# Second attention: one relu instruction over both PSUM banks of a pair, 128x2x256, with one wait and one signal, instead of one for each bank

## The chip, the cores and the metric

The kernel runs on one core of one Trainium2 chip. The metric is the time of one execution on the device in microseconds (us); lower is better. In this document TensorE is the matmul engine (PE in the rows, PEld its weight loads), VectorE is DVE, ScalarE is ACT, GpSimd is POOL and SyncE is SP. PSUM is the memory that matmuls write; its unit here is a bank, 512 fp32 values on each of 128 partitions.

## The reference, cut to what matters

Four layers run one after another on x of shape 16 x 512 x 128, each as x = x + layer(layernorm(x)): a first attention (causal, without softmax), a mixture-of-experts layer, a second attention, and the experts again. The change lies in the second attention, which begins like this:

```python
Q = proj(wq, bq); K = proj(wk, bk); V = proj(wv, bv)      # 16 heads of 8
scores = jnp.einsum('bhqd,bhkd->bhqk', Q, K) * scale       # 512 x 512 for each head
top_u = jax.lax.top_k(scores.max(axis=-1), u)[1]           # u = 6 queries of each head
```

Only the six queries with the largest row maximum go on to softmax and context. Nearly all the work of the stage is therefore the row maximum of 16 sequences x 16 heads x 512 queries over 512 keys.

## The kernel before, in words

Every engine has an instruction stream of its own, written out by hand; streams meet only at semaphore waits. The second attention runs `body` once for each of the 16 sequences b, and in it 32 steps n, one for each pair of (128 queries, two heads). A step uses one tile `pair[n % RING]` of two PSUM banks q = 0, 1, with RING = 3; a tile is used again three steps later. One step is:

- TensorE, `scores` (L1937 to L1948): for each bank q it waits until VectorE has signalled that bank's earlier content as read (`bmax_done`, three steps back), then writes 512 columns with a matmul on 32 rows of the array (L1947) and signals `bsc_done`. An fp32 matmul is two instructions in the profile, so a step has four.
- What lies in the two halves of a bank: the keys of `kTs` from column HALF on are 256 columns of k2 and then 256 columns of k1 - k2 (POOL makes the differences, L684). So the first half of a bank holds the scores of half of the keys, and the second half the differences of the other half's scores to them. The maximum of two scores is then first + relu(difference).
- ScalarE, `first_half_above` (L955 to L959): for each bank it waits for `bsc_done`, writes the relu of the second half (128x256) into the SBUF tile `rel[n % RING][:, q, :]` and signals `relu_done`. In the rows `rel` has the name pT, which is the memory it lies in.
- VectorE, `largest` (L1433 to L1441): for each bank it waits for `relu_done`, adds the first half of the bank and `rel`, takes the maximum along the row (L1439, two instructions in the profile: the custom reduction and the read of its accumulator into `smax`), and signals `bmax_done`, which frees the bank for TensorE.

Between the steps each stream has other work of the same and of neighbouring sequences at fixed places n. Those that matter here:

- VectorE: `residual` of an earlier sequence at n = 0 (L1497) and `route_ranks` after n = 3 (its last instruction writes `rank`, L1131).
- TensorE: after n = 5 `turn_largest`, which transposes the row maxima (L1953) and waits for `rank`; after n = 9 `project_q` (L1930); after n = 14 `select_x` (L1966); after n = 16 `select_q` (L1971); after n = 18 `selected_scores` (L1975); after n = 20, 22, 23, 24, 25, 26 and 29 seven more pieces (L1935, L1980, L1662, L1986, L1668, L1991, L1995); after n = 31 `scatter_context` (L2001).
- ScalarE: `largest` after n = 5 (L939), `masked_q` after each of n = 10 to 13 (L922, 128x512), `selected_x` after n = 14 (L948), and others.

The first body has no previous sequence and the last two no next one to work for, so these pieces are partly missing there; `each_four` strings the bodies together without a pause.

Of the kernel before, what the change touches and what calls it, by code (L numbers as in the profile page):

```python
# [10 lines left out]
ACT = mybir.ActivationFunctionType  # L11
# [11 lines left out]
SEQ = 512  # L23
# [24 lines left out]
RING = 3  # L48
PAIRS = TB * H // 2
HALF = SEQ // 2  # L50
# [9 lines left out]
def build(nc, w, out):  # L60
    ctx = ExitStack()
    with ctx:
# [6 lines left out]
        def sem(name):  # L69
            return ctx.enter_context(nc.semaphore(name))  # L70
# [140 lines left out]
        rel = [t[:, :, :].rearrange("p (q a) b -> p q (a b)", q=2) for t in pT[4:4 + RING]]  # L211
# [19 lines left out]
        pair = [ctx.enter_context(nc.psum_tensor(f"pair{i}", [P, 2, 512], F32)) for i in range(RING)]  # L231
# [13 lines left out]
        s = {n: sem(n) for n in names.split()}  # L245
# [534 lines left out]
        def _(act):  # L780
# [173 lines left out]

            def first_half_above(b, n):  # L955

                for q in range(2):
                    act.wait_ge(s["bsc_done"], 2 * (b * PAIRS + n) + q + 1)
                    act.activation(rel[n % RING][:, q, :], pair[n % RING][:, q, HALF:SEQ], ACT.Relu).then_inc(s["relu_done"], 1)  # L959

            def body(b, u, h, x, last=True, next=True, fetch=True, before=True):
                for n in range(PAIRS):
                    first_half_above(b, n)
                    if last and n == 5:
                        largest(b - 1)
                    if next and n == 7:
                        turned(b + 1 + B, "att", xnT)
                    if next and 10 <= n < 14:
                        masked_q(b + 1, 1 - h, range(n - 10, n - 9))
                    if last and n == 14:  # L970
                        selected_x(b - 1)
                    if last and n == 20:
                        selected_exp(b - 1)
                    if next and n == 20:
                        keys(b + 1, 1 - h)
                    if last and n == 22:
                        turned_exp(b - 1)
                    if before and n == 23:
                        turned(b - 2 + B, "ffn", xfT)
                    if last and n == 24:  # L980
                        context_x(b - 1)
                    if before and n == 26:
                        route_exp(b - 2 + B)
# [43 lines left out]
        def _(dve):  # L1027
# [405 lines left out]
            def largest(b, h, n):  # L1433

                t, j, a = n // (H // 2), n % (H // 2) // 2, n % 2
                for q in range(2):
                    dve.wait_ge(s["relu_done"], 2 * (b * PAIRS + n) + q + 1)
                    head = (2 * a + q) * GH + j
                    dve.tensor_tensor_reduce(out=rel[n % RING][:, q, :], in0=pair[n % RING][:, q, 0:HALF], in1=rel[n % RING][:, q, :],  # L1439
                                             scale=1.0, scalar=LOWEST, op0=ALU.add, op1=ALU.max,  # L1440
                                             accum_out=smax[h][:, t, head:head + 1]).then_inc(s["bmax_done"], 1)  # L1441
# [58 lines left out]
            def body(b, u, h, x, last=True, next=True, fetch=True, before=True):  # L1500
                for n in range(PAIRS):
                    largest(b, h, n)
                    if before and n == 0:
                        residual(b - 2)
# [664 lines left out]
```

## Time and profile before

| | us |
|---|---|
| median of 3 runs | 1378.17 |
| lowest and highest of the 3 runs | 1370.37 and 1379.9 |
| the profiled execution, its time | 1371.3 |
| the profiled execution, first to last instruction (span) | 1369.4 |
| second attention in it, first score matmul to last maximum | 480.67 to 1107.3 |

The profiled execution has 1.9 us outside its span. The page of the profile gives busy times of each engine, the chain of work that ended last, and the costliest groups of instructions. "Idle before" is the time in which an engine stood still just before an instruction, and the name behind the arrow is what ended it. Times in rows are us from the start of the span unless marked ns. A granted TensorE clock of 1.00 in a row is the full 2.4 GHz.

### The profile page before, as it was taken

What the parts mean: (1) busy time and instruction counts of PE and PEld (TensorE: products, weight loads), DVE (VectorE), ACT (ScalarE), POOL (GpSimd) and SP (SyncE); (2) the same over time, 40 slices, a digit from 0 to 9 for tenths busy, and PEclk for the clock granted to TensorE, in tenths of its full rate; (3) what the DMA queues carried; (4) which work ended last, traced back from release to release, by engine and by line L of the source; (5) the groups of instructions that cost most, each with busy time, mean ns of one, the idle gap of its engine ahead of it and who ended that gap; (6) DMA issues with size and microseconds to landing.
All of it is one profiled execution on the core that took longest, in us unless ns stands there. A gap on an engine that the chain in (4) does not pass through costs nothing.

```text
span 1369.4 us, 28269 instructions
## 1 busy us (share of the span) xinstructions
PE 1232.1 (90%) x8494; PEld 779.4 (57%) x8494; DVE 1040.6 (76%) x4462; ACT 759.4 (55%) x1907; POOL 832.5 (61%) x1238
## 2 busy tenths in 40 slices
PE   5999999999999999999999999999999999899100
PEld 2666655567898855545444545444454479799100
DVE  3899998996665478898999889989997756566322
ACT  3455443445756677675666677656666556556000
POOL 3247776677625134566777777767774445467776
PEclk9999999999999989998999899999999899999655
DMA  6855502013556400000101001020000125476522
GB/s 187 277 178 189 167 29 86 29 46 119 185 159 213 131 28 17 17 22 26 30 25 29 28 24 32 28 89 26 26 28 15 41 83 168 151 212 205 147 76 75
DMA packets 118695, 124.75 MB, mean 91 GB/s; under 512 B 15504, under 2 KB 108816, under 8 KB 118544
## 3 DMA queue, kind: packets, MB, share of 16 engines
q1 hardware_dynamic: 102160, 89.37, 20.6%
q0 software_dynamic: 16384, 33.59, 8.5%
q8 instruction: 68, 1.11, 0.3%
q14 instruction: 83, 0.68, 0.2%
HBM read 49.63 MB, written 73.27 MB: 90 GB/s over the span
## 4 chain that ended last, share of the span: by engine, by line
PE 74%; DVE 11%; POOL 5%; issue 4%; ACT 2%; DMA 2%; SPq 0%; ACTq 0%; POOLq 0%; DVEq 0%
PE pair L1947 26%; PE pair L1856 9%; POOL vmyg L585 5%; PE pair L1719 5%; PE bank L1743 4%; PE pair L1867 4%; DVE pT L1439 4%; PE pair L1845 2%; PE pair L1708 2%; PE bank L1668 2%; PE bank L1662 2%; PE pair L1689 1%; PE bank L1966 1%; PE pair L1729 1%; PE bank L1986 1%
## 5 line engine op out<-in xcount | busy, mean ns | idle before, releaser
L1947 PE MATMUL pair<-kT,apart 32*128 32x512 f32 x2048 | 460.2, 673 | 3.9 <-DVE smax L1439 2.5
L1439 DVE CUSTOM_DVE_ANT_0 pT<-pair,pT 128x256 f32<-128x256 f32 x1024 | 383.8, 416 | 76.0 <-ACT pT L959 70.8
L959 ACT ACTIVATE pT<-pair 128x256 f32<-128x256 f32 x1024 | 327.5, 397 | 197.5 <-PE pair L1947 194.5
L1947 PEld LDWEIGHTS pair<-kT,apart 32*128 32x128 f32 x2048 | 192.1, 191 | 127.9 <-DVE smax L1439 79.9
L585 POOL DMA_INDIRECT vmyg<-ybufA,slg x128 | 124.1, 969 | 100.0 <-DVE smax L1439 62.3
L1856 PE MATMUL pair<-xeT,unit_w 128*128 128x256 f32 x752 | 180.8, 384 | 0.0
L585 POOL DMA_INDIRECT vmyg<-ybufB,slg x128 | 122.7, 959 | 71.2 <-DVE smax L1439 33.5
L546 POOL DMA_INDIRECT dispB<-xnf,sli x128 | 128.5, 1004 | 57.1 <-issue 34.9
L546 POOL DMA_INDIRECT dispA<-xnf,sli x128 | 129.9, 1015 | 51.5 <-issue 30.1
L1152 DVE TENSOR_TENSOR pT<-pair,causal 128x1024 f32<-128x1024 f32 x128 | 151.2, 1213 | 12.9 <-PE pair L1719 12.1
L1322 DVE TENSOR_TENSOR hid<-sg,pair 128x512 f32<-128x512 f32 x96 | 64.8, 675 | 120.6 <-ACT sg L876 120.4
L1856 PEld LDWEIGHTS pair<-xeT,unit_w 128*128 128x128 f32 x752 | 137.5, 193 | 15.2
L1351 DVE SCALAR_TENSOR_TENSOR xs<-vmyg,wts,xs 128x128 f32<-128x128 f32 x248 | 80.8, 377 | 66.6 <-DMA vmyg<-ybufB,slg 55.1
L1867 PE MATMUL pair<-unit_w,hid 128*128 128x128 f32 x752 | 100.4, 276 | 7.3 <-DVE ye L1331 7.3
L1867 PEld LDWEIGHTS pair<-unit_w,hid 128*128 128x128 f32 x752 | 97.9, 191 | 15.8 <-DVE hid L1322 6.7
L883 ACT ACTIVATE unit_w<-f_w 128x384 f32 x156 | 73.2, 515 | 49.9 <-PE pair L1867 47.7
L876 ACT ACTIVATE sg<-pair 128x512 f32<-128x512 f32 x96 | 56.6, 589 | 50.4 <-PE pair L1856 50.0
L1439 DVE DVE_READ_ACCUMULATOR2_ANT smax<- 128x1 f32 x1024 | 82.5, 81 | 0.0
L1719 PE MATMUL pair<-apart,kT 32*128 32x512 f32 x512 | 77.6, 651 | 1.7 <-DVE pT L1152 1.7
L1331 DVE COPY ye<-pair 128x512 f32<-128x512 f32 x96 | 64.5, 672 | 8.8 <-PE pair L1867 5.2
L1743 PE MATMUL bank<-pT,vmyg 128*32 128x128 f32 x2048 | 70.7, 280 | 0.0
L483 POOL TENSOR_SCALAR lnv<-mv 128x4 f32<-128x4 f32 (+1 forms) x51 | 12.0, 235 | 87.9 <-DVE mv L1050 85.7
(232 smaller groups left out, 1946.1 us busy)
## 6 DMA issues: line engine op xcount, KB each, us to landing
dispB<-zeros SPq DMA_DIRECT2D x16, 1408.0 KB
apart<-dispA SPq DMA_DIRECT2D x94, 128.0 KB
apart<-dispB SPq DMA_DIRECT2D x94, 128.0 KB
ybufA<-ye SPq DMA_DIRECT2D x46, 256.0 KB
ybufB<-ye SPq DMA_DIRECT2D x46, 256.0 KB
dispA<-zeros SPq DMA_DIRECT2D x33, 128.0 KB
xs<-in_x SPq DMA_DIRECT2D x16, 256.0 KB, 3.1
out<-xs SPq DMA_DIRECT2D x15, 256.0 KB, 2.6
```

What stands on the lines that cost most here:

```text
L546: pool.indirect_dma_start(out=area, out_offset=bass.IndirectOffsetOnAxis(ap=sli[h][:, K * j + k:K * j + k + 1], axis=0), in_=xnf[g % NF][: ...
L585: pool.indirect_dma_start(out=yg[h][:, j, :], out_offset=None, in_=ybuf[second(g)], in_offset=bass.IndirectOffsetOnAxis(ap=slg[h][:, j:j + ...
L883: last = act.activation(unit_w[g % NX][:, u, :], f_w[:, bass.ds(ex[u], 1), :].rearrange("p a n -> p (a n)"), ACT.Copy)
L959: act.activation(rel[n % RING][:, q, :], pair[n % RING][:, q, HALF:SEQ], ACT.Relu).then_inc(s["relu_done"], 1)
L1152: dve.tensor_tensor(pTd[n % NG][:, :, :], pair[1 + n % 2][:, :, :].rearrange("p q (j t) -> p (q j) t", j=GH), causal[:, :].unsqueeze(1).to ...
L1351: last = dve.scalar_tensor_tensor(out=xb, in0=yg[h][:, K * j + k, :], scalar=wts[:, bass.ds((b * TB + j) * K + k, 1)], in1=xb, op0=ALU.mul ...
L1439: dve.tensor_tensor_reduce(out=rel[n % RING][:, q, :], in0=pair[n % RING][:, q, 0:HALF], in1=rel[n % RING][:, q, :], scale=1.0, scalar=LOW ...
L1719: pe.matmul(bank[4 + g][:, :].rearrange("p (j t) -> p j t", j=GH), kTs[h][at, c * P:(c + 1) * P], apart[h][at, :, c * P:(c + 1) * P], star ...
L1743: last = pe.matmul(bank[1][at:at + QG, c * P:(c + 1) * P], vm[:, c, j * P + at:j * P + at + QG], pT[c % 2 * NG + g][:, j, :], start=(c == ...
L1856: last = pe.matmul(bank[3 + 2 * h + k][:, u * UR:(u + 1) * UR], unit_w[r][:, u, k * D:(k + 1) * D], xeT[h][:, UT * u:UT * (u + 1), :].rear ...
L1867: last = pe.matmul(bank[7][:, j * D:(j + 1) * D], hid[h][:, j, :], unit_w[r][:, j // UT, 2 * D:3 * D], start=True, stop=True)
L1947: pe.matmul(pair[n % RING][:, q, :], apart[h][at, j, t * P:(t + 1) * P], kTs[h][at, HALF:], start=True, stop=True).then_inc(s["bsc_done"], 1)
```

## The change

On ScalarE the two waits and two activations of a step become one wait for both banks (`bsc_done` at its second count) and one activation over both banks, 128 partitions x 2 x 256, with one signal. On VectorE the wait for `relu_done` moves out of the loop over q: one wait for the step, then the two reductions. `relu_done` counts steps in place of banks. Nothing else changes: matmuls, reductions, `bmax_done` for each bank and the ring of three stay as they are.

```diff
             def first_half_above(b, n):
 
-                for q in range(2):
-                    act.wait_ge(s["bsc_done"], 2 * (b * PAIRS + n) + q + 1)
-                    act.activation(rel[n % RING][:, q, :], pair[n % RING][:, q, HALF:SEQ], ACT.Relu).then_inc(s["relu_done"], 1)
+                act.wait_ge(s["bsc_done"], 2 * (b * PAIRS + n) + 2)
+                act.activation(rel[n % RING][:, :, :], pair[n % RING][:, :, HALF:SEQ], ACT.Relu).then_inc(s["relu_done"], 1)
...
             def largest(b, h, n):
 
                 t, j, a = n // (H // 2), n % (H // 2) // 2, n % 2
+                dve.wait_ge(s["relu_done"], b * PAIRS + n + 1)
                 for q in range(2):
-                    dve.wait_ge(s["relu_done"], 2 * (b * PAIRS + n) + q + 1)
                     head = (2 * a + q) * GH + j
```

## Rows read from the trace of the kernel before

**Rows 1.** The page: span, and each engine's busy us, share, instructions.

```profile
span 1369.4 us, 28269 instructions
...
PE 1232.1 (90%) x8494; PEld 779.4 (57%) x8494; DVE 1040.6 (76%) x4462; ACT 759.4 (55%) x1907; POOL 832.5 (61%) x1238
```

**Rows 2.** Busy time by engine in one steady body: PE, PEld, DVE, ACT, POOL, clock.

```profile
706.70:744.98 38.28, 38.19 (x198) 19.24 (x197) 35.00 (x193) 26.28 (x78) 28.41 (x39) 1.00 0.10 28
```

**Rows 3.** Waits over 0.15 us, whole second attention: total us, times, longest.

```profile
ACT pT L959 <- PE pair L1947: 194.5, 210, 4.3
...
PEld pair L1947 <- DVE smax L1439: 79.9, 157, 2.0
...
DVE pT L1439 <- ACT pT L959: 70.8, 100, 3.1
```

**Rows 4.** The same wait of VectorE in the first body and the last.

```profile
DVE pT L1439 <- ACT pT L959: 7.5, 12, 1.6
...
DVE pT L1439 <- ACT pT L959: 10.8, 11, 3.1
```

**Rows 5.** ScalarE's instructions by shape: busy us, mean ns, idle before.

```profile
L959 ACT ACTIVATE pT<-pair 128x256 f32<-128x256 f32 x1024 | 327.5, 397 | 197.5 <-PE pair L1947 194.5
...
L876 ACT ACTIVATE sg<-pair 128x512 f32<-128x512 f32 x92 | 55.0, 598 | 45.9 <-PE pair L1856 45.4 <-issue 0.2
...
L876 ACT ACTIVATE sg<-pair 128x256 f32<-128x256 f32 x4 | 1.5, 384 | 4.5 <-PE pair L1856 4.5
```

**Rows 6.** Timeline at n = 0 of that body: start, us, engine, line.

```profile
707.85 1.48 ACT L959 ACTIVATE pT<-pair 128x256 f32<-128x256 f32 x4 [1.76 <-PE pair L1947]
708.27 0.42 DVE L1439 CUSTOM_DVE_ANT_0 pT<-pair,pT 128x256 f32<-128x256 f32 x1 [0.54 <-ACT pT L959]
...
708.62 0.42 DVE L1439 CUSTOM_DVE_ANT_0 pT<-pair,pT 128x256 f32<-128x256 f32 x1
```

**Rows 7.** Chain that ended last, between n = 3 and n = 6.

```profile
712.21 0.23 DVE rank L1131
...
712.49 0.60 PE bank L1953 x4
```

**Rows 8.** Timeline at n = 6.

```profile
714.18 1.21 ACT L959 ACTIVATE pT<-pair 128x256 f32<-128x256 f32 x4 [0.46 <-PE pair L1947]
...
714.60 0.42 DVE L1439 CUSTOM_DVE_ANT_0 pT<-pair,pT 128x256 f32<-128x256 f32 x1 [0.80 <-ACT pT L959]
```

**Rows 9.** Timeline, ScalarE and VectorE, at n = 10 and 11.

```profile
718.69 0.66 ACT L959 ACTIVATE pT<-pair 128x256 f32<-128x256 f32 x2 [1.52 <-PE pair L1947]
...
719.24 0.78 ACT L922 ACTIVATE apart<-bank,qbias,inturn 128x512 f32<-128x512 f32 x1
...
719.90 0.67 ACT L959 ACTIVATE pT<-pair 128x256 f32<-128x256 f32 x2
...
720.33 0.42 DVE L1439 CUSTOM_DVE_ANT_0 pT<-pair,pT 128x256 f32<-128x256 f32 x1
```

**Rows 10.** Timeline at n = 14 and 15.

```profile
722.21 0.38 PE L1966 MATMUL bank<-pT,xnb 128*128 128x128 f32 x1
...
724.45 1.21 ACT L959 ACTIVATE pT<-pair 128x256 f32<-128x256 f32 x4
...
724.87 0.42 DVE L1439 CUSTOM_DVE_ANT_0 pT<-pair,pT 128x256 f32<-128x256 f32 x1
```

**Rows 11.** Timeline at n = 19.

```profile
728.97 1.21 ACT L959 ACTIVATE pT<-pair 128x256 f32<-128x256 f32 x4 [1.54 <-PE pair L1947]
729.38 0.42 DVE L1439 CUSTOM_DVE_ANT_0 pT<-pair,pT 128x256 f32<-128x256 f32 x1
```

**Rows 12.** Timeline at n = 26 and at the next body's n = 0.

```profile
738.86 0.66 ACT L959 ACTIVATE pT<-pair 128x256 f32<-128x256 f32 x2 [1.39 <-PE pair L1947]
...
739.27 0.43 DVE L1439 CUSTOM_DVE_ANT_0 pT<-pair,pT 128x256 f32<-128x256 f32 x1 [0.88 <-ACT pT L959]
...
746.56 0.42 DVE L1439 CUSTOM_DVE_ANT_0 pT<-pair,pT 128x256 f32<-128x256 f32 x1 [0.54 <-ACT pT L959]
```

## The prediction

> **What bounds the kernel now.** The page first: 1369.4 us of span, VectorE busy 76% of it and ScalarE 55% [rows 1]. These are averages over four layers, so the second view is one body of the second attention alone. In its 38.28 us TensorE shows 38.19 busy at the full granted clock, VectorE 35.00 and ScalarE 26.28 [rows 2]. VectorE is nearly full and ScalarE is not (69%). TensorE's figure must not be taken as a bound: two steps that have their banks ready share the array, so the same work could take less.
>
> The third view, the waits, shows a ring. TensorE's weight loads waited 79.9 us for VectorE's maxima (a bank not yet read), ScalarE waited 194.5 us for score matmuls, and VectorE 70.8 us, 100 times, for the relu [rows 3]. So a bank goes matmul, relu, reduction and back, and each engine in it at times waits for the one before. The view has no other wait of VectorE. Whether such a standstill lies on the path that sets the end has to be read place by place, and that is done below.
>
> **What the change does to one step.** It removes 512 activations, waits and signals on ScalarE and 512 waits on VectorE; it adds no matmul, reduction or transfer. VectorE's two reductions stay .35 us apart [rows 6], which is the reduction and its accumulator read, so the wait taken away there gives nothing.
>
> The new instruction, 128x2x256, is not in the trace. Nearest are two shapes on one line, 128x256 at 384 ns and 128x512 at 598 ns; today's relu, 397 ns on average, is the first shape [rows 5]. The 256 further elements cost 598 - 384 = 214 ns. I take .60 us. From above it is bounded by the .66 that two relus take today [rows 9], and if a second bank cost as much as a second instruction, by 2 x .385 = .77; from below by .385 + .21, since the elements are all still read.
>
> First effect, a gain: on ScalarE a step holds the engine from 718.69 until the next instruction begins at 719.24, .55 us [rows 9]. The second of two activations starts before the first has ended: two of .385 to .40 take .66, so some .12 overlap. The new one lets the next start after .60 - .12 = .48 to .49, so .06 is saved in each step.
>
> Second effect, a loss: today the first reduction starts .42 after the first relu (707.85 to 708.27 [rows 6]; the same at n = 6, 15, 19 and 26 [rows 8, 10 to 12]), while the second relu runs beside it. Now it starts .60 + .03 after the instruction begins: **.21 later**. Where VectorE releases the two banks .35 apart and the matmuls follow at that distance, the one wait for both banks adds that .35 too.
>
> The trace shows ScalarE unsaturated and VectorE waiting for it. The Trainium skill, Perfetto Trace Analysis, section Optimizing Scalar/DVE Operations, says that grouping into larger operations helps if the engine is saturated, and that if ScalarE or VectorE aren't saturated but cause bubbles on other engines, breaking instructions up may let work complete sooner. By the first half the kernel would gain ScalarE's time, by the second it would lose what is worked out below; the rows show the second case.
>
> **Where .21 counts.** I follow one body from its n = 0 (VectorE 708.27) to the next n = 0 (746.56 [rows 12]), 38.29 us, and ask at each wait what released it, and how far that has moved already.
>
> 1. n = 0: VectorE waits .54 [rows 6] for matmuls that stand behind `scatter_context`. Late: .21. From here VectorE works without a real pause to `rank`, which releases TensorE's L1953 [rows 7].
> 2. n = 6: its matmuls follow L1953 directly; VectorE waits .80 [rows 8]. Total .42.
> 3. n = 11: the second reduction of n = 6 frees the bank for n = 9, after it come `project_q` and n = 10, whose relu starts at 718.69 after an idle 1.52. Then ScalarE itself is the bound: relu, `masked_q`, relu [rows 9]. Here .06 is gained, so .15 is added. Total .57. At n = 12 to 14 ScalarE gains further, but by then VectorE, moved by .57, is itself the later one.
> 4. n = 15: the second reduction of n = 11 frees the bank for n = 14, behind it stands `select_x` (722.21), behind that n = 15, whose relu starts at 724.45 [rows 10]. Total .78.
> 5. n = 19: the reductions of n = 15 free the banks of n = 18, then `selected_scores`, then n = 19, for which ScalarE had been idle 1.54 [rows 11]. VectorE started just as the relu ended, so all .21 is late. Total .99.
> 6. n = 26: the second reduction of n = 19 frees n = 22; after that TensorE is the bound, with another piece after nearly every step, and VectorE waits .88 [rows 12]. Total 1.20. The reductions of n = 26 to 28 free the banks of n = 29 to 31, `scatter_context` follows, and the ring closes at the next n = 0.
>
> So a body becomes 5 x .21 + .15 = **1.20 us** longer, 3%. Eleven bodies are of this kind (the fourth to the fourteenth): 11 x 1.20 = 13.2 us.
>
> The other five miss some of this work. By the waits view the first has 12 waits of VectorE for the relu and the last 11 [rows 4], the three between them 7, 5 and 10: 45 of the 100. The eleven have 55, and 13.2 / 55 = .24 us for each; 45 x .24 = 10.8. Sum **24.0 us**. A second count agrees roughly: 100 waits x .21 = 21.
>
> No other queue is passed by anything that moves. POOL's gathers and scatters are released by VectorE's maxima, so they shift with the bodies; experts before and after are untouched.
>
> The profiled execution took 1371.3 us, 1.9 beyond its span: 1371.3 + 24.0 = **1395.3 us**. Its time lies 6.9 below the median shown (1378.17); against that the same sum would be 1402.
>
> **The rivals.**
>
> *Hidden anyway.* VectorE is busy 35.00 of 38.28 [rows 2], and most steps reach it with the relu long done; if the matmul order sets the pace, lateness ends in the next wait. For it: only 100 of 512 steps show a wait over .15 [rows 3]. Against: the waits are released by matmuls that themselves waited for VectorE, so they move along. If only the crossings at n = 0 and n = 6 hold: 16 x .42 = 6.7, so 1378 us; if none, 1371.
>
> *Faster: ScalarE is the bound at n = 10 to 13.* There .06 is gained in four steps of 15 bodies: 15 x 4 x .06 = 3.6 us, 1367.7. It decides if all first-bank lateness is hidden and VectorE still follows ScalarE at n = 14. Even .06 in all 512 steps would give only 31 us, and ScalarE's 194.5 us of waiting [rows 3] exclude most of that. The Trainium skill, ScalarE: Activation LUTs, section What ACT_TABLE_LOAD costs, gives 186 ns + 0.833 ns for each element and about 93 ns of overlap; by it one instruction saves 93 ns against two, an estimate of 48 us of ScalarE time in all. The trace agrees on the slope (214 ns for 256).
>
> *Slower by far: the ring runs in step.* Where no other work lies between, the banks are released .35 apart, and each turn through three steps pays .21 + .35 = .56. If all 100 waits paid that: 56 us, 1427. The first body has such a stretch; in the eleven others the waits that count follow a piece of TensorE work, after which both banks start together.
>
> *The instruction is dearer.* At .66 a crossing costs .275, at .77 it costs .385: 24.0 x .275 / .21 = 31, 1402; 24.0 x .385 / .21 = 44, 1415.
>
> **How the numbers follow.** My forecast, with its bounds on the instruction's price (1395 to 1415), has .72; hidden anyway .17; in step .07; faster through ScalarE .04. The range goes from 1378 (two crossings a body) to 1415 (the dear instruction). A measurement of this kernel can tell about 1% from no change, 14 us. Slower by more: nearly all of the forecast and the in-step case, .76. Within: hidden anyway, the gain of ScalarE (3.6 us is 0.3%), and a forecast half as large, .20. Faster by over 1% needs a gain of 14 us that no row shows: .04.
>
> **What would show it.** Right: the new instruction at about .60 us; the body of 38.28 at about 39.5; VectorE's waits for the relu longer and more often, with the first reduction .63 after the relu starts; ScalarE's busy time for L959 down from 327.5 to about 307. TensorE's waits for VectorE's maxima go up as well. Wrong: bodies of 38.3 us, in which the longer wait is paid back by a shorter one at the next place; or a VectorE that waits no longer than today, since the relu then came early enough.

## The result and the profile after

The changed kernel took 1413.49 us (median of 4 runs, 1411.02 to 1426.4), the kernel before 1379.04 in the same comparison (4 runs, 1370.37 to 1382.7). The ratio is 1.0294, 95% interval 1.0251 to 1.0337: slower by 2.5 to 3.4%, and by 34.5 us if the medians are compared, which is the lower end of that. Ratios, here and below, leave out the few runs that took over 1.5% longer than the fastest of their kernel; medians are of all runs. The forecast was slower, 1395.3 us. That is 24.0 above the profiled execution before but only 16 above the median of 1379.04, so against the median the loss was about twice the forecast.

The page of the changed kernel, first its span and the busy time of each engine, then the three groups of the ring (line, engine, operation, busy us and mean ns, idle before):

```profile
span 1413.9 us, 27757 instructions
...
PE 1276.8 (90%) x8494; PEld 796.6 (56%) x8494; DVE 1043.5 (74%) x4462; ACT 730.7 (52%) x1395; POOL 830.9 (59%) x1238
...
L1946 PE MATMUL pair<-kT,apart 32*128 32x512 f32 x2048 | 497.4, 708 | 4.4 <-DVE smax L1438 2.9
L1438 DVE CUSTOM_DVE_ANT_0 pT<-pair,pT 128x256 f32<-128x256 f32 x1024 | 387.1, 417 | 115.3 <-ACT pT L958 112.2
L958 ACT ACTIVATE pT<-pair 128x512 f32<-128x512 f32 x512 | 296.3, 601 | 271.3 <-PE pair L1946 270.0
```

The new instruction takes 601 ns, as estimated from [rows 5]. ScalarE is busy 28.7 us less than before (759.4 [rows 1] to 730.7) and waits more. Its time for this line is 296.3 us and not the 307 forecast: 512 instructions of 601 ns would be 308, but some overlap. VectorE's work is the same; its wait for the relu has grown from 70.8 us [rows 3] to 112.2. The waits view of the second attention counts how often (total us, times, longest):

```profile
ACT pT L958 <- PE pair L1946: 270.0, 312, 4.3
DVE pT L1438 <- ACT pT L958: 112.2, 141, 3.0
PEld pair L1946 <- DVE smax L1438: 86.5, 165, 1.5
```

The windows view gives the first three bodies and one later body (length, then busy us of PE, PEld, DVE, ACT, POOL, then the granted TensorE clock as a share of 2.4 GHz, the DMA engines' busy share and GB/s):

```profile
482.61:521.54 38.93, 38.32 (x136) 20.43 (x137) 26.39 (x140) 21.59 (x37) 13.40 (x16) 0.69 0.08 21
521.54:563.59 42.05, 41.40 (x180) 21.36 (x180) 31.64 (x161) 25.70 (x46) 14.97 (x17) 0.84 0.05 13
563.59:605.11 41.52, 41.04 (x194) 20.28 (x193) 35.12 (x188) 24.49 (x46) 18.91 (x23) 0.96 0.05 14
850.85:890.63 39.78, 39.58 (x198) 19.59 (x197) 35.02 (x194) 24.55 (x46) 28.57 (x40) 1.00 0.09 27
```

The last line answers to [rows 2]: at the full clock a body takes 39.78 us in place of 38.28, 1.5 more (1.20 was forecast). The first lines show what the forecast has no word of. The same three bodies in the kernel before:

```profile
480.67:513.89 33.22, 32.96 (x136) 18.11 (x137) 25.81 (x140) 24.37 (x69) 13.42 (x16) 0.85 0.09 24
513.89:550.10 36.21, 35.22 (x180) 19.08 (x180) 31.29 (x161) 27.21 (x79) 15.10 (x17) 1.00 0.06 16
550.10:588.23 38.13, 38.05 (x193) 19.21 (x192) 34.26 (x188) 26.31 (x78) 18.95 (x23) 1.00 0.06 15
```

They took 33.22, 36.21 and 38.13 us, with clocks of 0.85, 1.00 and 1.00; now they take 38.93, 42.05 and 41.52, and TensorE ran a good part of them at half clock (1.2 GHz). The whole stage grew by 42.8 us, from 626.6 to 669.4.

Within the body at full clock the crossings (the places where a late relu makes VectorE start later) can be read one by one. The timeline at its n = 0, n = 6 and the next body's n = 0:

```profile
852.06 0.60 ACT L958 ACTIVATE pT<-pair 128x512 f32<-128x512 f32 x1 [1.60 <-PE pair L1946]
852.69 0.42 DVE L1438 CUSTOM_DVE_ANT_0 pT<-pair,pT 128x256 f32<-128x256 f32 x1 [0.80 <-ACT pT L958]
...
858.65 1.08 ACT L958 ACTIVATE pT<-pair 128x512 f32<-128x512 f32 x2 [0.51 <-PE pair L1946]
859.28 0.42 DVE L1438 CUSTOM_DVE_ANT_0 pT<-pair,pT 128x256 f32<-128x256 f32 x1 [1.01 <-ACT pT L958]
...
892.48 0.42 DVE L1438 CUSTOM_DVE_ANT_0 pT<-pair,pT 128x256 f32<-128x256 f32 x1 [0.80 <-ACT pT L958]
```

From the start of the relu to the reduction it is .63 now (852.06 to 852.69) against .42 [rows 6]: the forecast .21. VectorE's wait at n = 0 went from .54 to .80, at n = 6 from .80 to 1.01 [rows 6, 8], though what comes before had already moved. Measured from the start of the first relu of the body, VectorE's first reduction shifted by:

| place | forecast, total | measured, total |
|---|---|---|
| n = 0 | .21 | .21 |
| n = 6 | .42 | .47 |
| n = 11 | .57 | .66 |
| n = 15 | .78 | .92 |
| n = 19 | .99 | 1.18 |
| n = 26 | 1.20 | 1.43 |

The steps are the ones named, but most are .25 to .26 and not .21. Where the other .04 to .05 lies is seen at n = 26, where nothing but one step's four matmuls stands before the relu. First the kernel before, then the changed one:

```profile
737.70 1.13 PE L1947 MATMUL pair<-kT,apart 32*128 32x512 f32 x4
738.86 0.66 ACT L959 ACTIVATE pT<-pair 128x256 f32<-128x256 f32 x2 [1.39 <-PE pair L1947]
```

```profile
883.09 1.13 PE L1946 MATMUL pair<-kT,apart 32*128 32x512 f32 x4
884.29 0.60 ACT L958 ACTIVATE pT<-pair 128x512 f32<-128x512 f32 x1 [1.46 <-PE pair L1946]
```

The matmuls take 1.13 in both. The relu follows their start after 1.16 (738.86 - 737.70) before and 1.20 (884.29 - 883.09) now. Only what the relu waits for has changed: both banks in place of the first (one_wait below, with narrow relus, has 1.20 too). So the wait for the second bank costs .04, and a crossing costs .21 + .04.

### The profile page after: what moved, and what is told of

It reads as the page before. It is cut to its first block, busy times and chain, and to the rows that moved or that the text cites. A ratio compares the mean times of both kernels' runs of the same rounds, so it can differ in the third digit from the quotient of the medians.

```text
span 1413.9 us, 27757 instructions
## 1 busy us (share of the span) xinstructions
PE 1276.8 (90%) x8494; PEld 796.6 (56%) x8494; DVE 1043.5 (74%) x4462; ACT 730.7 (52%) x1395; POOL 830.9 (59%) x1238
## 4 chain that ended last, share of the span: by engine, by line
PE 74%; DVE 11%; POOL 4%; issue 4%; ACT 3%; DMA 2%; SPq 1%; ACTq 0%; POOLq 0%; DVEq 0%
PE pair L1946 28%; PE pair L1855 8%; PE pair L1718 5%; POOL vmyg L585 4%; PE bank L1742 4%; PE pair L1866 4%; DVE pT L1438 3%; PE pair L1844 2%; PE bank L1667 2%; PE pair L1707 2%; PE bank L1661 2%; PE pair L1688 1%; PE bank L1965 1%; DVE xs L1350 1%; PE bank L1974 1%
## 5 line engine op out<-in xcount | busy, mean ns | idle before, releaser
L1946 PE MATMUL pair<-kT,apart 32*128 32x512 f32 x2048 | 497.4, 708 | 4.4 <-DVE smax L1438 2.9
L1438 DVE CUSTOM_DVE_ANT_0 pT<-pair,pT 128x256 f32<-128x256 f32 x1024 | 387.1, 417 | 115.3 <-ACT pT L958 112.2
L958 ACT ACTIVATE pT<-pair 128x512 f32<-128x512 f32 x512 | 296.3, 601 | 271.3 <-PE pair L1946 270.0
L1946 PEld LDWEIGHTS pair<-kT,apart 32*128 32x128 f32 x2048 | 205.7, 201 | 146.7 <-DVE smax L1438 86.5
L1151 DVE TENSOR_TENSOR pT<-pair,causal 128x1024 f32<-128x1024 f32 x128 | 151.3, 1214 | 13.2 <-PE pair L1718 12.6
```

What stands on the lines that cost most here:

```text
L958: act.activation(rel[n % RING][:, :, :], pair[n % RING][:, :, HALF:SEQ], ACT.Relu).then_inc(s["relu_done"], 1)
L1151: dve.tensor_tensor(pTd[n % NG][:, :, :], pair[1 + n % 2][:, :, :].rearrange("p q (j t) -> p (q j) t", j=GH), causal[:, :].unsqueeze(1).to ...
L1946: pe.matmul(pair[n % RING][:, q, :], apart[h][at, j, t * P:(t + 1) * P], kTs[h][at, HALF:], start=True, stop=True).then_inc(s["bsc_done"], 1)
```

## Experiments

The theory after this: (a) the late first reduction, .25 a crossing at six places of a body, is the change's direct cost; (b) the half clock is a cost of its own. Rivals: the wait for both banks, the wide instruction as such, a fixed cost for each step, and for (b) chance.

All are shown as edits of the kernel before, if not said otherwise. The ratio of each is to runs of the kernel before taken beside it, whose medians lay between 1371.68 and 1379.04 us. "Stage" is the length of the second attention in the profiled execution and its mean granted clock. "At full clock" is worked out as stage x (1 - .69 x (1 - clock)). The factor comes from the kernel before, from the body after the one in [rows 2], the next one, and the stretch in them at half clock:

```profile
744.98:785.89 40.91, 40.82 (x198) 20.34 (x198) 36.08 (x198) 26.21 (x78) 29.84 (x41) 0.90 0.10 30
785.89:825.13 39.24, 39.12 (x199) 19.63 (x198) 34.16 (x189) 26.11 (x78) 27.74 (x38) 0.97 0.08 25
777.70:787.90 10.20, 10.20 (x40) 4.99 (x38) 6.78 (x47) 3.33 (x12) 5.47 (x6) 0.50 0.08 27
```

The two bodies hold 10.2 us at half clock and took 40.91 + 39.24 in place of 2 x 38.30, 3.55 us more, so about .35 us for each us at half clock. A mean clock c means 2 x (1 - c) of the time at half clock, and 2 x .345 is the .69. The factor was measured at one place of the body; as will be seen at joint_first_three, the last column is good to some 3 us.

| kernel | median us | ratio to before (95%) | body at clock 1.00 | stage, clock | stage at full clock |
|---|---|---|---|---|---|
| before | 1379.04 | | 38.28 | 626.6, .956 | 607.6 |
| changed | 1413.49 | 1.0294 (1.0251 to 1.0337) | 39.78 | 669.4, .911 | 628.3 |
| before_again | 1376.89 | 1.0002 (.9965 to 1.0040) | 38.29 | 635.1, .936 | 607.1 |
| one_signal | 1413.85 | 1.0264 (1.0208 to 1.0320) | 39.96 | 672.2, .912 | 631.4 |
| one_wait | 1387.05 | 1.0105 (1.0033 to 1.0177) | 38.56 | 637.8, .938 | 610.5 |
| joint_short | 1374.10 | .9987 (.9956 to 1.0018) | 38.29 | 642.1, .921 | 607.1 |
| joint_at_waits | 1418.64 | 1.0344 (1.0279 to 1.0409) | 40.11 | 671.2, .915 | 631.8 |
| joint_elsewhere | 1381.87 | 1.0059 (1.0023 to 1.0096) | 38.40 | 636.7, .941 | 610.8 |
| joint_first_three | 1396.75 | 1.0208 (1.0154 to 1.0263) | 38.29 (later ones) | 647.6, .921 | 612.3 |
| joint_later | 1404.77 | 1.0232 (1.0166 to 1.0297) | 40.10 | 654.3, .948 | 630.8 |
| grouped | 1341.35 | .9766 (.9720 to .9812) | 36.97 | 595.4, .977 | 586.0 |
| grouped_joint | 1377.36 | 1.0017 (.9985 to 1.0050) | 38.30 | 632.1, .956 | 612.9 |
| turn_early | 1375.38 | .9960 (.9910 to 1.0010) | 37.98 | 618.5, .953 | 598.4 |
| grouped_spread | 1340.51 | .9780 (.9739 to .9820) | 36.97 | 595.3, .980 | 587.1 |

**before_again.** No edit.

> The kernel before, unchanged, to see how much of the time moves with the granted clock when nothing is changed. If the lower granted clock of the changed kernel (0.916 over the span against 0.939 in the profiled run before) belongs to the change: clock 0.935 to 0.945, 1370 to 1383 us, bodies of 38.3 us at full clock. If it is chance from run to run: clocks down to 0.91 here as well, and times up to about 1400 us.

Ten runs lay between 1368.63 us (clock over the span .939) and 1383.19 (.924): 14.6 us for .015 of mean clock, 9.7 for each .01. So the profiled execution of the kernel before, 1371.3 at .939, was among its fastest. The changed kernel's four runs had .905 to .925, median .919, against .931 here: below, with hardly an overlap. (The .931 itself lies below the .935 to .945 expected.) The lower clock belongs to the change and isn't chance. At 9.7 us for each .01 it makes some 12 of the 34.5 us.

**one_signal.**

```diff
 for q in range(2):
     act.wait_ge(s["bsc_done"], 2 * (b * PAIRS + n) + q + 1)
-    act.activation(...).then_inc(s["relu_done"], 1)
+    done = act.activation(...)
+done.then_inc(s["relu_done"], 1)
...
+dve.wait_ge(s["relu_done"], b * PAIRS + n + 1)
 for q in range(2):
-    dve.wait_ge(s["relu_done"], 2 * (b * PAIRS + n) + q + 1)
```

> VectorE's half of the change alone: two relu instructions, each with its own wait, but only the second one signals, and VectorE waits once for a step. The first reduction then starts .66 + .03 after the first relu begins, .27 late in place of .21, and ScalarE saves nothing. Theory 'late first reduction': at least as slow as the changed kernel, bodies at full clock 39.8 to 40.5 us, 1411 to 1435 us, granted clock over the span 0.90 to 0.92. Rival 'wait for both banks' and rival 'wide instruction' (the loss comes from ScalarE waiting for the second bank, or from reading two banks in one instruction): near the kernel before, 38.3 to 38.7 us a body, 1371 to 1390 us.

A later body at full clock (columns as in the windows above):

```profile
731.29:771.25 39.96, 39.76 (x198) 19.63 (x198) 35.43 (x194) 26.44 (x78) 28.63 (x39) 1.00 0.09 27
```

39.96 us, 1.7 more than before and .2 more than the changed kernel, with two narrow instructions and a wait for each bank. The reduction starts .69 after the relu in place of .42, .27 late, and six times .27 is 1.6. The whole loss comes without the wide instruction, from the late signal alone.

**one_wait.**

```diff
+act.wait_ge(s["bsc_done"], 2 * (b * PAIRS + n) + 2)
 for q in range(2):
-    act.wait_ge(s["bsc_done"], 2 * (b * PAIRS + n) + q + 1)
     act.activation(...).then_inc(s["relu_done"], 1)
```

> ScalarE's wait alone: it waits for both banks before the first relu, then runs two relu instructions with a signal each, and VectorE waits for each bank as before. Theory 'late first reduction': at the places that count both banks' matmuls end together, so bodies stay at 38.3 to 38.5 us; only stretches in which the banks come .35 apart lose, 2 to 8 us in all: 1372 to 1388 us, clock 0.93 to 0.94. Rival 'wait for both banks': most of the loss is here, 39.5 us a body, 1400 us or more. Rival 'wide instruction': no change.

```profile
672.92:711.48 38.56, 38.47 (x198) 19.30 (x197) 35.01 (x194) 26.30 (x78) 28.61 (x40) 1.00 0.10 29
```

.27 a body, a little above the expected 38.3 to 38.5: six crossings at .04 to .05, the wait for the second bank seen above. The wait for both banks is a sixth of the loss and not the most of it.

**joint_short.** The changed kernel with 2 x 128 columns in its instruction; the relu of the other columns is left out.

```diff
-act.activation(rel[n % RING][:, :, :], pair[n % RING][:, :, HALF:SEQ], ACT.Relu).then_inc(s["relu_done"], 1)
+act.activation(rel[n % RING][:, :, 0:P], pair[n % RING][:, :, HALF:HALF + P], ACT.Relu).then_inc(s["relu_done"], 1)
```

> The changed kernel with its one instruction cut to 2 x 128 columns, so that it takes as long as one relu before (.385); the relu of the other half of the columns is left out. One wait, one instruction and one signal over two banks remain, only the lateness is gone. Theory 'late first reduction': bodies of 38.0 to 38.4 us, granted clock back at 0.935 or more, 1365 to 1382 us. Rivals 'wait for both banks' and 'wide instruction' (one instruction over two banks does the harm): 39.5 us a body or more and 1395 us or more still. If the clock falls for a reason of its own, it stays at 0.92 here and the time is 1385 to 1395 us.

Its relu group, and a body at full clock:

```profile
L958 ACT ACTIVATE pT<-pair 128x256 f32<-128x256 f32 x512 | 187.3, 385 | 331.0 <-PE pair L1946 330.5
```

```profile
588.02:626.31 38.29, 38.20 (x199) 19.30 (x198) 35.05 (x194) 18.17 (x46) 27.77 (x38) 1.00 0.09 25
```

With one instruction over two banks, but as short as one relu before, the loss is gone: 38.29. That it is gone to the last hundredth is luck, for two effects cancel. The wait for both banks is still there, and the body should be as long as that of one_wait, 38.56. It isn't, because ScalarE's time counts at one place, n = 10 and 11, where a relu, `masked_q` and the next relu stand in a row. First one_wait, then joint_short (start, us, and VectorE's first reduction of n = 11):

```profile
685.06 0.66 ACT L959 ACTIVATE pT<-pair 128x256 f32<-128x256 f32 x2 [1.49 <-PE pair L1947]
686.27 0.67 ACT L959 ACTIVATE pT<-pair 128x256 f32<-128x256 f32 x2
686.70 0.42 DVE L1439 CUSTOM_DVE_ANT_0 pT<-pair,pT 128x256 f32<-128x256 f32 x1 [0.22 <-ACT pT L959]
```

```profile
600.16 0.38 ACT L958 ACTIVATE pT<-pair 128x256 f32<-128x256 f32 x1 [1.77 <-PE pair L1946]
601.10 0.38 ACT L958 ACTIVATE pT<-pair 128x256 f32<-128x256 f32 x1
601.52 0.42 DVE L1438 CUSTOM_DVE_ANT_0 pT<-pair,pT 128x256 f32<-128x256 f32 x1
```

The relu of n = 11 follows that of n = 10 after 1.21 us in one_wait and after .94 here: .27 gained, and VectorE no longer waits there. So of the 8.1 us less of ScalarE's time in the body (18.17 against 26.28 [rows 2]) .27 are worth something, and the rest nothing. The width of the instruction costs nothing by itself: from its start to the reduction it is .42, as before.

**joint_at_waits and joint_elsewhere.** The wide instruction in some steps only, VectorE waiting for each bank as before.

```diff
+if n in WAITED:   # 0, 6, 11 to 15, 17 to 19, 25 to 27; "not in" for joint_elsewhere
+    act.wait_ge(s["bsc_done"], 2 * (b * PAIRS + n) + 2)
+    act.activation(rel[n % RING][:, :, :], pair[n % RING][:, :, HALF:SEQ], ACT.Relu).then_inc(s["relu_done"], 2)
+    return
```

> The joint instruction only at the 13 steps of a body (n = 0, 6, 11 to 15, 17 to 19, 25 to 27) where VectorE waits for the relu or starts within .2 us of its end; the other 19 steps as before. Theory 'late first reduction, place by place': nearly the whole loss, bodies at full clock of 39.6 to 39.9 us against 38.29, granted clock of the span 0.915 to 0.928, 1403 to 1420 us. Rival 'a fixed cost for each step': 13/32 of the loss, bodies of 38.9 us and about 1393 us.

> The other half: the joint instruction at the 19 steps of a body where VectorE comes late to the relu, the 13 steps at which it waits as before. Theory 'late first reduction, place by place': bodies at full clock of 38.2 to 38.4 us; a loss only in the first two bodies and the last, where VectorE waits at other places too; 1372 to 1386 us, clock 0.927 to 0.938. Rival 'a fixed cost for each step': 19/32 of the loss, 39.2 us a body and about 1397 us.

```profile
806.83:846.94 40.11, 39.85 (x199) 19.64 (x198) 35.06 (x194) 25.69 (x65) 28.60 (x40) 1.00 0.09 27
```

```profile
748.98:787.38 38.40, 38.31 (x198) 19.31 (x197) 35.19 (x194) 25.03 (x59) 27.76 (x38) 1.00 0.09 27
```

The 13 steps where VectorE waits for the relu or starts close behind it carry the loss (first fence, 40.11; 39.6 to 39.9 was expected), the 19 others hardly any (second, 38.40). There is no fixed cost for each step. The first kernel is .3 slower in a body than the changed one, and joint_later below too: in both, the relu began .06 later after its matmuls (1.26 against 1.20). They share a signal that counts two and a wait for each bank on VectorE; which of them does it was not tried.

**joint_first_three and joint_later.** The same edit with `b < 3` and with `b >= 3` as its condition.

> The joint instruction in the first three of the 16 bodies only, all others as in the kernel before. In the trace of the changed kernel these three are 14.9 us longer than before (38.93, 42.05 and 41.52 against 33.22, 36.21 and 38.13), with 41 us at the half clock against 10. If that belongs to the change: 10 to 17 us longer than before, 1387 to 1395 us, and about 30 to 45 us at the half clock in these bodies. If lateness costs the same everywhere and the half clock there was chance: 3 x 1.5 = 4.5 us, 1380 to 1383 us.

> The complement of joint_first_three: the joint instruction in bodies 4 to 16, the first three as in the kernel before. If the change loses its time in two separate ways (1.5 us in every later body through the late first reduction, and a longer stretch at the half clock at the beginning, where joint_first_three lost 18.7 us in its trace), this kernel loses 13 x 1.5 = 19.5 us, a little more where the clock falls more often in the longer bodies: 1390 to 1402 us, bodies of 39.8 us at full clock, first three as before (33 to 34, 36.2, 38.1 us), clock 0.925 to 0.932. If the low clock of the changed kernel comes from the later bodies, it is at 0.92 here too, and the time at 1405 us or more.

The first three bodies of joint_first_three:

```profile
478.19:517.35 39.16, 38.11 (x136) 19.35 (x137) 26.06 (x140) 21.77 (x38) 13.41 (x16) 0.77 0.07 21
517.35:560.57 43.22, 42.57 (x181) 22.55 (x181) 31.53 (x161) 25.59 (x46) 15.09 (x17) 0.81 0.05 13
560.57:604.47 43.90, 43.09 (x193) 21.80 (x192) 36.12 (x192) 24.14 (x46) 18.91 (x23) 0.89 0.05 13
```

They take 126.3 us in place of 107.6. By their clocks 44 us of them ran at half clock (before: 10), although the edit touches nothing of TensorE. At full clock the three bodies are some 7 us longer by their own times (126.3 - 44 x .35 against 107.6 - 10 x .35), and the whole stage is 612.3 - 607.6 = 4.7 longer. That is 1.6 to 2.4 for each of the three: the late first reduction at about its usual price, the 1.8 of this edit. The median clock over the span was .919 in its four runs, as low as in the changed kernel, against .937 in the kernel before taken beside it; in joint_later, with 13 bodies changed, it was .931 against .935. So the change loses in two ways. In every body it is late, and in the first three it also puts TensorE at half clock for longer.

The other profiles bear this out. The time at half clock in the first three bodies, by their granted clocks:

| kernels | us at half clock |
|---|---|
| late there: changed, one_signal, joint_at_waits, joint_first_three, grouped_joint | 41, 44, 31, 44, 34 |
| one_wait (.04 late) | 20 |
| the eight others (joint_short, .04 late too, among them) | 7 to 10 |

From the fourth body on the profiles don't part in this way: 79 us in the changed kernel, 44 in the kernel before, but 72 in before_again and 94 in joint_short, which isn't slower. So of the 65 us more at half clock in the profile of the changed kernel (119 against 55), the 31 of the first three bodies are the change's; the others can be chance.

joint_first_three, at 1396.75 us, lies just above the 1387 to 1395 expected, and joint_later, at 1404.77, above its 1390 to 1402. joint_later lost 23 us at full clock, its excess of .3 a body (4 us) among them. The two ratios, 2.1 and 2.3%, sum to more than the whole change's 2.9%. Those 4 us are .3% of it; the rest, 1.2%, is a little more than the three intervals explain, and where it comes from isn't shown.

What TensorE did before it fell, in the changed kernel and then in the kernel before:

```profile
488.00:498.00 10.00, 9.75 (x45) 4.95 (x44) 6.63 (x37) 7.52 (x14) 6.62 (x7) 0.99 0.19 48
498.00:535.00 37.00, 36.97 (x118) 19.82 (x114) 24.13 (x125) 17.46 (x30) 9.61 (x12) 0.50 0.04 10
```

```profile
484.00:494.00 10.00, 10.00 (x51) 5.06 (x47) 7.25 (x41) 8.40 (x24) 7.22 (x8) 1.00 0.17 43
494.00:501.00 7.00, 7.00 (x26) 4.87 (x24) 5.35 (x30) 5.64 (x16) 0.49 (x1) 0.53 0.07 17
```

In the 10 us before the fall it ran 45 matmuls in place of 51 (the x behind its busy time). Both kernels fall at this place; the changed one then stays at half clock for 37 us and not for 7, with 118 matmuls, 32 in 10 us. That a TensorE which gets its banks late does less in a given time, and that a longer stretch at half clock follows, agrees with the table above; what exactly sets the length of the stretch isn't shown.

**grouped.** From the fourth to the tenth body the clock fell at one place only, 32.5 to 33.9 us after a body's start: in the fourth and the eighth body of the kernel before, in the fifth and the eighth of the changed one. That is where TensorE runs single steps between pieces of other work (n = 22 to 26). Two pieces were moved by one step, so that steps run in twos there:

```diff
-if before and n == 23:
+if before and n == 22:
     ...
     turn(b - 2 + B, "ffn", xnf[(b - 2 + B) % NF])
...
-if before and n == 25:
+if before and n == 26:
     logits(b - 2 + B, bank[0])
```

> The kernel before with two pieces of TensorE's other work moved by one step: the transposes of xnf from after n = 23 to after n = 22, logits from after n = 25 to after n = 26, so that steps 23 and 24, and 25 and 26, run side by side on the array. Theory: in n = 22 to 26 TensorE alone sets the pace, because single steps between pieces take 1.06 us where two together take 1.3, and VectorE pays for it at n = 25 (.42) and n = 26 (.88). Then bodies get 0.5 to 1.3 us shorter, 37.0 to 37.8 us, and the granted clock, which in the steady bodies fell 32.3 to 33.9 us after their start, falls less often: 0.935 to 0.95, 1345 to 1370 us. Rival 'VectorE's own work is the bound there': bodies stay at 38.2 us or more, or get longer because logits come later, 1370 to 1385 us.

One body, and eight bodies in a row (the fourth to the eleventh):

```profile
808.55:845.52 36.97, 36.88 (x199) 19.40 (x198) 34.92 (x194) 26.12 (x78) 28.66 (x39) 1.00 0.10 30
```

```profile
586.82:883.32 296.50, 294.99 (x1579) 155.06 (x1578) 279.90 (x1542) 208.77 (x624) 228.17 (x311) 1.00 0.10 29
```

In the kernel before these eight bodies lie from 588.23 to 902.55: 314.32 us at a mean clock of .97. A body is 1.31 shorter, nothing of its work is gone, and in the 296.5 us the clock didn't fall once. The median is 1341.35 us: 2.3% faster than before and 72 us below the changed kernel. That is more than expected (37.0 to 37.8 us a body, 1345 to 1370 us). This is the version that beats both.

**turn_early.** The first of the two moves alone.

> One of the two moves of the kernel 'grouped' alone: the transposes of xnf after n = 22, logits left after n = 25. Steps 23 and 24 then run together, 25 and 26 don't. If VectorE's wait of .88 at n = 26 is what the pace hangs on, .3 us a body is won (VectorE's wait at n = 25 goes from .42 to .1, the same shift stays at n = 26), bodies of 37.9 to 38.1 us and 1362 to 1374 us; if bringing logits out from between 25 and 26 alone was worth nothing, all of it, 37.0 us a body and 1341 us.

Bodies of 37.98, .3 won as expected; the other 1.0 needs `logits` out from between steps 25 and 26, where VectorE waited .88 [rows 12]. Its ten runs lay between 1357.3 and 1380.09 us at clocks of .944 to .922, and their median, 1375.38, just above the 1362 to 1374 expected, so the time alone (.9960) would have told nothing; the body at full clock does.

**grouped_joint.** The same two moves in the changed kernel.

> The same two moves in the changed kernel. If the late first reduction costs .21 to .26 at each crossing that is left, the joint relu still costs 1.0 to 1.5 us a body against the kernel 'grouped' (one crossing, n = 25 and 26, may be hidden), 16 to 24 us plus what the clock takes: 1370 to 1400 us. If the loss needed TensorE to be the bound in n = 22 to 26, it shrinks to 0.5 us a body or less.

38.30 us a body, 1.33 more than grouped, and 27 us for the stage at full clock (612.9 - 586.0). The first five crossings cost .21 to .26 each as before, the sixth, now at n = 25, only .10 (n = 26 no longer waits). So the late first reduction does not need TensorE's single steps. In the steady bodies the clock stays at 1.00 here as well, so the falls there belong to TensorE's order and not to the relu; in the first two bodies it is at half clock for 34 us, much as in the changed kernel.

**grouped_spread.** grouped, and ScalarE's `masked_q` spread out.

```diff
-if next and 10 <= n < 14:
-    masked_q(b + 1, 1 - h, range(n - 10, n - 9))
+if next and n in (10, 12, 13, 16):
+    masked_q(b + 1, 1 - h, ((10, 12, 13, 16).index(n),))
```

> The kernel 'grouped', with ScalarE's masked_q after n = 10, 12, 13 and 16 in place of 10, 11, 12 and 13. It tests whether ScalarE is a bound at n = 10 to 14, as step 3 of the prediction has it. If so, VectorE's waits at n = 11 (.17) or n = 14 (.15) go, and a body becomes 0.1 to 0.3 us shorter, 36.7 to 36.9 us, 1335 to 1341 us. If VectorE's own work or TensorE sets the pace there, bodies stay at 36.97 us and the time at 1341 us.

No gain: 36.97 both times. VectorE's wait of .15 at n = 14 went away and came back at n = 15, which had waited .12 and now waits .39: there TensorE's `select_x` sets the pace. The edit leaves `masked_q` behind n = 10, and VectorE's wait at n = 11 stayed (.18), so it says nothing of the place where joint_short gained.

## Why the prediction was right and wrong

**Right: the mechanism, its places and its direct size.** That VectorE pays for a first reduction .21 late, at six crossings of a body, each released by an instruction that had itself been late. one_signal, one_wait, joint_short and the pair joint_at_waits and joint_elsewhere leave none of the rivals named for it. The sum of 24.0 us stands against 628.3 - 607.6 = 20.7 at full clock, but partly by errors that cancel. A steady body was mis-sized at 1.20 for 1.50: most of the difference is the .04 for the second bank, at each crossing, which the prediction didn't have (it reckoned the wait for both banks as free where their matmuls start together). The eleven bodies still cost 13.4 together, as forecast (13.2), because two of them, the eleventh and the twelfth, in which TensorE has further pieces, are hardly longer than before (80.6 us together at full clock against 80.2). The five other bodies were put too high with 10.8: by their own times at full clock they cost some 7, the first three 4.3 of it.

**Wrong: the sum ended there.** The step that failed is "1371.3 + 24.0 = 1395.3": it holds the granted clock fixed, so that the clock is a term of nothing, and it gives no reason. The row it argued from shows a body at clock 1.00, and the page before has slices below 9 tenths, which were passed over (the second line is the changed kernel's):

```profile
PEclk9999999999999989998999899999999899999655
PEclk9999998999999959999899899969889899999655
```

In the traces the stage grew by 42.8 us, of which some 21 are lateness and 22 are time at half clock (about 119 us of it in place of 55). By the medians it is 34.5, some 21 of lateness and 12 to 13 of clock; the 31 us more at half clock in the first three bodies, at .35 each, make 11 of these. The second fault of the step is its base. The profiled execution had a clock of .939, near the top of what the kernel before shows; the prediction saw that it lay 6.9 us low and left it at that, and in the comparison it was 7.7. The clock is the reason for both errors, and they point the same way. The time came out at the upper end of the range, which had been drawn for a dearer instruction, a reason that did not occur.

**Rivals.** Hidden anyway: fell, as no crossing is paid back within a body. Faster through ScalarE: fell as a forecast, but the mechanism is real at one place. The .06 did come at n = 11 (.19 added there in place of .25), and joint_short, with far less of ScalarE's time, gains .27 there; against six crossings that is little. In step: the first three bodies of the changed kernel pay 1.4 each at full clock, no more than the others. The dearer instruction: no, 601 ns.

**The rule.** The Trainium skill, Perfetto Trace Analysis, section Optimizing Scalar/DVE Operations, says that grouping can improve throughput if the engine is saturated, and that breaking instructions up may let work end sooner where an engine isn't saturated but makes others wait. The runs agree with the second half: ScalarE was busy 69% of a body, grouping its two instructions freed 28.7 us of its time in all, and the kernel lost 34.5.

## What to carry to other kernels

Between two engines that hand tiles round in a ring, what an instruction delivers first matters, and not what it costs its engine: merging two instructions and their signals saves the producer's time and delays the consumer by the second half, at each place where the consumer waits. Follow one period of the schedule from wait to wait and add up; that gives the direct cost well. Wait for each input by itself: the wait for both banks alone cost .04 at each place. Then ask what the delay does to the granted clock, take the base from the median and not from the one profiled run, and compare stretches at equal clock.

## What the runs showed of the hardware

- Two banks' matmuls run side by side on different rows of the array; an instruction that waits for both began .04 us later than one that waits for the first (1.20 and 1.16 us from the matmuls' start), in one_wait, where nothing else was changed, as in the changed kernel.
- The time of one and the same kernel follows its mean granted clock, 9.7 us for each .01 between .924 and .939, and a change on ScalarE and VectorE alone lowers that clock: .931 to .919 by the medians. In the five profiles in which the first three bodies get their reductions late, TensorE is at half clock there for 31 to 44 us, in eight others for 7 to 10.
- Moving two pieces of TensorE's work by one step, with no work taken away, kept the clock at 2.4 GHz through eight bodies in which it had fallen to 1.2 GHz twice.
